# First graph sorted without the nodes' own loops: 440 tiles of edges for 464

## The reference

```python
edge_index = jnp.stack([src, dst])        # 53125, loops among them
# L0: twice GATv2 (4 heads of 64, then 1 of 256), once more with loops appended
src = concatenate([edge_index[0], loops]); dst = concatenate([edge_index[1], loops])
m = xl[src] + xr[dst]; logits = einsum('ehc,hc->eh', leaky_relu(m, 0.2), att)
ex = exp(logits - segment_max(logits, dst)[dst])
out = segment_sum(ex / segment_sum(ex, dst)[dst] * xl[src], dst) + bias
# L1: relations, no loops appended
agg = segment_sum(hx[edge_type, src], dst)
# L2: twice GCN, loops appended: deg counts them
m = (h @ W)[src] * (dinv[src] * dinv[dst])[:, None]; out = segment_sum(m, dst) + b
# L3: 8 heads of 32 with edge attributes, no loops appended
```

## Time and profile before

| what | value |
|---|---|
| median of 3 runs | 9657.73 us (9654.73 to 9668.22) |
| the profiled execution's own time | 9654.4 us |
| its span | 9652.8 us |
| instructions | 96508 |
| mean granted TensorE clock | 0.758 |
| POOL busy, indirect DMAs | 5442.8 us, 56% of the span |
| HBM traffic | 106 GB/s over the span |

### The profile page before, as it was taken

How to read it: one execution, slowest core, us unless ns; L and a number is a source line. 1 busy time by engine, 2 the same in 40 slices (tenths; PEclk the granted TensorE clock), 3 DMA queues, 4 the chain that set the end, 5 groups by cost and what they waited for, 6 DMA issues and landing times. The chain is left out here.

```text
span 9652.8 us, 96508 instructions
## 1 busy us (share of the span) xinstructions
PE 5709.5 (59%) x28237; PEld 4044.7 (42%) x28237; DVE 5273.2 (55%) x11304; ACT 1819.3 (19%) x5534; POOL 5442.8 (56%) x5200
## 2 busy tenths in 40 slices
PE   4866666376665678654687122444444678645496
PEld 4766555254554444443444012333333434334364
DVE  8796566596667852444211196444444455489222
ACT  2444111372110011000111001001000122245110
POOL 2777777374776675576477302774771157546202
PEclk9777889698898989777788556666665555579698
DMA  0001455363555503333456705554552234445311
GB/s 20 4 4 27 126 163 160 98 184 104 161 163 147 148 9 96 99 99 79 130 157 134 77 10 190 149 149 114 150 149 72 70 102 133 119 126 152 108 32 59
DMA packets 570475, 1030.73 MB, mean 107 GB/s; under 512 B 148601, under 2 KB 341795, under 8 KB 568734
## 3 DMA queue, kind: packets, MB, share of 16 engines
q0 software_dynamic: 244320, 586.94, 24.2%
q1 hardware_dynamic: 325657, 437.62, 14.0%
HBM read 812.61 MB, written 211.21 MB: 106 GB/s over the span
## 5 line engine op out<-in xcount | busy, mean ns | idle before, releaser
L171 PE MATMUL ps<-g,oh 128*128 128x256 bf16 (+4 forms) x6496 | 1600.7, 415 | 1313.5 <-issue 796.1
L175 POOL DMA_INDIRECT g<-xl_g,xsrc x1392 | 1531.0, 1100 | 735.8 <-issue 368.0
L171 PEld LDWEIGHTS ps<-g,oh 128*128 128x128 f32 (+1 forms) x6496 | 1143.9, 183 | 1770.0 <-issue 1116.8
L175 POOL DMA_INDIRECT g<-gcn,xsrc x928 | 944.9, 1018 | 855.2 <-SPq L131 571.6
L1188 DVE TENSOR_TENSOR h<-h,ps 128x256 f32 x1392 | 586.3, 421 | 1078.5 <-PE ps L171 903.0
L171 PE MATMUL ps<-g,ident 128*128 128x256 f32 x1856 | 566.6, 459 | 449.8 <-DMA g<-xl_g,xsrc 449.6
L175 POOL DMA_INDIRECT wide<-gat_rows,xs x576 | 575.6, 999 | 356.1 <-issue 174.6
L181 POOL DMA_INDIRECT tab_m<-x,m_addr x441 | 493.0, 1118 | 288.8 <-DVE m_addr L612 154.8
L181 POOL DMA_INDIRECT tab_n<-n_pay,n_addr x537 | 537.0, 1000 | 203.5 <-issue 163.3
L171 PEld LDWEIGHTS ps<-g,ident 128*128 128x128 f32 x1856 | 396.4, 224 | 569.9 <-DMA g<-xl_g,xsrc 510.9
L175 POOL DMA_INDIRECT g<-hx_rel,xtyp x464 | 475.2, 1024 | 252.6 <-issue 141.2
(11 more groups left out here) (499 smaller groups left out, 10700.9 us busy)
## 6 DMA issues: line engine op xcount, KB each, us to landing
kept_g<-g SPq DMA_DIRECT2D x232, 256.0 KB, 2.2
g<-kept_g SPq DMA_DIRECT2D x232, 256.0 KB, 3.2
rowb<-dst_rows_m SPq DMA_DIRECT2D x87, 512.0 KB, 4.5
kept_h<-gk SPq DMA_DIRECT2D x116, 264.0 KB, 2.1
g<-kept_h SPq DMA_DIRECT2D x116, 264.0 KB, 2.8
hx_rel<-tb SPq DMA_DIRECT2D x200, 128.0 KB, 1.8
g<-xl_g,xsrc POOLq DMA_INDIRECT x1392
rowb<-dst_rows_n SPq DMA_DIRECT2D x36, 512.0 KB, 4.2
```

The costliest lines, as they stand in the source:

```text
L171: return k.nc.tensor.matmul(out, lhsT, rhs, start=start, stop=stop, skip_group_check=True)
L175: return k.nc.gpsimd.indirect_dma_start(out=out, out_offset=None, in_=table, in_offset=bass.IndirectOffsetOnAxis(ap=index, axis=0), bounds ...
```

## The change

The loops that L0 and L2 append are no longer edges of m: J is 416 and T 440. What they contributed is computed per node:

- GCN sums start from the node's own row: `gcn_table` keeps dinv x h in `h` and `seg_sum(begun=True)` adds to it, without its memset. The degree is the count plus 1.
- GATv2: `gat_tables` keeps xl in the output tile and writes xl + xr over xT; `gatv2_logits` makes the nodes' own logits of it, in 20 pieces of VectorE work per layer, one in every fifth group of tiles. The softmax now stores each edge's maximum, not the difference; `numerators` takes the place of `from_rows` and also keeps that maximum M per edge; `seg_mean` sums H more columns with it (weighed by the numerators, or with one head in the one-hots), gets the node's maximum by division, and joins both shares (`with_own`).
- The softmax of m works on TS = 448 columns, 8 of them with a target that matches none, in 32 windows of 14 tiles per head (29 of 16 before), 112 with one head (116), 16 with eight.
- `dlR` and `loopneg` are gone.

The second graph's lists stay; its softmax goes through `numerators` too.

```diff
 def both_graphs(k, a, x):
-    m = EdgeList(k, "m", 441, 464, 8)
+    m = EdgeList(k, "m", 416, 440, 8)
+    k.TS = 448
...
 # seg_softmax, sync
-            sp.dma_start(dram2.rearrange("(q e) -> q e", q=Q), x[0:Q, :])...
+            sp.dma_start(dram2.rearrange("(q e) -> q e", q=Q), d[0:Q, 0:n])...
 # seg_softmax, vector
-            vec.tensor_tensor(x[0:Q, :], x[0:Q, :], d[0:Q, 0:n], ALU.subtract)...
...
-    from_rows(k, dram2, H * T, L, ACT.Exp)
+    numerators(k, dram2, H * T, L, M, M is not None and H > 1)
 # numerators, ACT and VectorE (new; loads and transposes as from_rows)
+            for i in range(n + 2):
+                if i < n and M is not None:
+                    act.wait_ge(turned.sem, turned.at(i + 1))
+                    act.copy(M[:, cols(i)], k.ps[i % 4][:, 0:widths[i]])...
+                if i >= 2:
+                    act.wait_ge(shifted.sem, shifted.at(a + 1))
+                    act.activation(L[:, cols(a)], L[:, cols(a)], ACT.Exp)...
+            for i in range(n + 4):
+                if i < n:
+                    vec.tensor_tensor(L[:, cols(i)], L[:, cols(i)], maxima, ALU.subtract)...
+                if i >= 4 and weigh:
+                    vec.tensor_tensor(M[:, cols(a)], M[:, cols(a)], L[:, cols(a)], ALU.mult)
 # seg_sum
-            step(k, vec.memset(acc[:, :], 0.0))
+            if not begun:
+                step(k, vec.memset(acc[:, :], 0.0))
 # seg_mean, ACT, per group
+                if own is not None:
+                    act.copy(g[:, rows_at(t, S), D + H:V], mv[:, t:t + S, :])
 # seg_mean, with_own, after eleven small operations and one Exp
+            if H == 1:
+                for b in range(NB):
+                    vec.wait_ge(own_weighed.sem, own_weighed.at(b + 1))
+                    vec.scalar_tensor_tensor(out=o3[:, b, :], in0=a3[:, b, 0:D], scalar=both[:, 0, b, :],
+                                             in1=o3[:, b, :], op0=ALU.mult, op1=ALU.add)
+                return
+            for h in range(H):
+                for s, v3 in enumerate((a3, o3)):
+                    v = v3[:, :, c * h:c * (h + 1)]
+                    step(k, vec.tensor_tensor(v, v, bc(both[:, s, :, h:h + 1], [128, NB, c]), ALU.mult))
+            vec.tensor_tensor(o3, o3, a3[:, :, 0:D], ALU.add)
 # gatv2_logits, vector
+                if i % 5 == 4 and i // 5 < 20:
+                    own_logits(i // 5 // 4, i // 5 % 4)
+        def own_logits(s, part):
+            v = sums[:, :, 640 * s:640 * (s + 1)]
+            if part == 0:
+                step(k, vec.scalar_tensor_tensor(out=v, in0=v, scalar=0.2, in1=v, op0=ALU.mult, op1=ALU.max))
+            elif part == 1:
+                chain(k, vec.tensor_tensor, v4, v4, bc(att...), ALU.mult)
+            else:
+                chain(k, vec.tensor_reduce, own[...], v[:, part - 2, :]..., AX, ALU.add)
 # gat_tables, vector, per block of the right-hand projection
+                    vec.tensor_tensor(xT[:, :, 128 * i:128 * i + 128], h3[:, i, :]..., ps(NB + i)..., ALU.add)
 # gcn_table, vector, per block
-                    vec.scalar_tensor_tensor(out=rest[:, i % 4, :], in0=k.ps[2 + i % 4][:, 0:D],
-                                             scalar=dinv[:, i:i + 1], in1=buf[:, i % 6, 0, :], ...)
+                    vec.tensor_scalar(h3[:, i, :], k.ps[2 + i % 4][:, 0:D], dinv[:, i:i + 1], None, ALU.mult)
+                    vec.tensor_tensor(rest[:, b % 4, :], h3[:, b, :], buf[:, b % 6, 0, :], ALU.subtract)
 # l3_logits
-            chain(k, vec.tensor_tensor, Lv, Lv, bc(k.loopneg[:, :].unsqueeze(1), [128, 8, T]), ALU.add)
```

More of the change, by code:

```diff
@@ L303, in split_digits @@
         made = sum(len(lists) for _, lists, _, _ in graphs) + 1
+        with_loops = [e.name for e, _, loops, _ in graphs if loops is not None]
         def sync():
@@ L318, in pool @@
             for e, _, loops, _ in graphs:
+                if loops is None:
+                    continue
                 nc.gpsimd.wait_ge(loaded[e.name].sem, loaded[e.name].at(len(parts[e.name])))
@@ L334, in vector @@
             vec.wait_ge(cleared.sem, cleared.at(made))
-            for i, (e, _, _, attr) in enumerate(graphs):
+            for e, _, loops, attr in graphs:
                 vec.wait_ge(loaded[e.name].sem, loaded[e.name].at(len(parts[e.name])))
-                vec.wait_ge(looped.sem, looped.at(2 * i + 2))
+                if loops is not None:
+                    vec.wait_ge(looped.sem, looped.at(2 * with_loops.index(e.name) + 2))
                 digits(e, cols[e.name], ti[e.name], attr)
@@ L734, in vector @@
             vec.tensor_copy(k.attr[:, :, :], p[:, :, 4:7])
[L735 to L738 removed]
+            vec.scalar_tensor_tensor(out=k.dlA[:, :], in0=k.blk[:, :], scalar=-128.0, in1=p[:, :, 0], op0=ALU.mult,
+                                     op1=ALU.add)
         sync()
@@ L934, in scans @@
             step(k, vec.tensor_copy(cc[0:Q, 0:1], k.ps[0][0:Q, 0:1]))
-            chain(k, vec.tensor_tensor_scan, o, g, i_, cc[0:Q, 0:1], ALU.add, ALU.max)
+            if back:
+                after_steps(k, vec)
+                vec.tensor_tensor_scan(o, g, i_, cc[0:Q, 0:1], ALU.add, ALU.max).then_inc(maxima_made.sem,
+                                                                                          maxima_made.up())
+            else:
+                chain(k, vec.tensor_tensor_scan, o, g, i_, cc[0:Q, 0:1], ALU.add, ALU.max)
         def vector():
@@ L1135, in is_kept, with seg_sum @@
     return t % 4 >= 2
-def seg_sum(k, T, table, rows, idx, dl, offs, acc, W=D, parts=1, S=8, R=4):
+def seg_sum(k, T, table, rows, idx, dl, offs, acc, W=D, parts=1, S=8, R=4, begun=False):
     nc = k.nc
@@ L1204, in seg_sum, with seg_mean @@
         fence(k)
-def seg_mean(k, T, table, dl, ex, out, H, kept, W=D, least=1.0e-30):
+def seg_mean(k, T, table, dl, ex, out, H, kept, W=D, least=1.0e-30, M=None, own=None):
     nc = k.nc
     vec, act, pe, gp, sp = nc.vector, nc.scalar, nc.tensor, nc.gpsimd, nc.sync
-    S, R, V = 4, 4, D + H
+    S, R, V = 4, 4, D + H * (1 if own is None else 2)
     G = T // S
+    TS = ex.shape[1] // H
     on_act = {1: 0, 4: 2, 8: 1}[H]
@@ L1228, in seg_mean @@
         ones_set = k.sem("ones_set")
+        shifted, powered = k.sem("logits_shifted"), k.sem("numerators_made")
+        shares, own_weighed = k.sem("shares_made"), k.sem("own_weighed")
+        a3 = acc[:, 0, :].rearrange("p (b c) -> p b c", b=NB)
+        o3 = out.rearrange("p (b c) -> p b c", b=NB)
+        c = D // H
         def rows_at(t, n=1):
@@ L1376, in of, with gatv2_logits @@
         return self.oh[:, (t // 4) % self.R, 128 * (t % 4):128 * (t % 4) + 128]
-def gatv2_logits(k, T, table, xr3, att, H, L, kept):
+def gatv2_logits(k, T, table, xr3, att, H, L, kept, sums, own):
     nc = k.nc
@@ L1456, in vector @@
         def vector():
+            vec.memset(Lv[:, T:, :], 0.0)
             for i in range(4):
@@ L1488, in gatv2_logits, with gat_tables @@
         fence(k)
-def gat_tables(k, xT, Wl, Wr, att, xr3, attb, table):
+def gat_tables(k, xT, Wl, Wr, att, xr3, attb, table, h3):
     nc = k.nc
@@ L1559, in gat_layer @@
 def gat_layer(k, name, xT, Wl, Wr, att, H, acc):
-    T = k.T
+    T, TS = k.T, k.TS
     table = k.dram("xl_" + name, (3200, D))
@@ L2657, in gcn_table @@
         loaded, projected, taken = k.sem("weights_loaded", 16), k.sem("projected"), k.sem("projected_kept")
-        part_a, part_v = k.sem("parts_kept_a"), k.sem("parts_kept_v")
+        first, second, third = k.sem("first_parts_kept"), k.sem("second_parts_kept"), k.sem("third_parts_kept")
+        rests = k.sem("rests_made")
         stored = k.ring("table_stored", 6)
```

308 lines of the change are left out of this document (184 added, 124 removed).

## The result

| | before | changed |
|---|---|---|
| median | 9658.75 us (9654.73 to 9668.22, 4 runs) | 9343.6 us (9337.72 to 9347.09, 4 runs) |
| profiled execution (span) | 9654.4 us (9652.8) | 9347.09 us (9345.8) |
| mean granted TensorE clock | 0.758 | 0.759 |

The ratio is 0.9672, with a 95% interval of 0.9655 to 0.9688: the change is faster by 3.3%, 315 us by the medians, 307 by the profiled executions. 9365 was forecast, with 9333 to 9398 as the range. Four kernels of the experiments ran first in a period when the chip granted TensorE less clock (0.706 on average for 0.759), in which the kernel before took 11229.75 us.

The account below looks back on a forecast made before the run. The prediction took POOL, issuing one indirect DMA per tile, to bound the first graph's tile stages, with no engine bounding the whole span. Its terms summed to -292 us from 9657.7, giving 9365 us, range 9333 to 9398.

Parts of the forecast that it names:

- Start: Before layer 0: 25 fewer scatters and a first address 9 us earlier bring the first gather to about 1002.6, -42.5 us.
- Logits: Layer 0's two logits passes: 24 fewer tiles at 1.413 us each, -67.8; nodes' own VectorE pieces slow POOL, +11.
- Sums, means, last logits: First graph's passes: 24 fewer tiles at POOL's price; plain sums -95.4, means' gathers -51.6, last layer's logits -36 us.
- Rival (e): First graph's stages: latency, not POOL's rate, sets a group's pace, so they win a third less, 70 us: 9435; chance 0.04.
- Softmaxes: All softmaxes: new windows cut load waits and stores, subtractions go, numerators cost +3, +2.5, +1, +1; sum -56 us.
- Tails: Behind the means' last tiles: joining the nodes' own shares costs +17.8 with four heads, +8.2 with one, +26 us together.
- Tables: Projections and GCN tables: extra VectorE operations cost +7 in the second layer and +6.5 per GCN table, +20 us.
- the fixed price of the product: Logits passes: two-SBUF-input VectorE work, judged from the product r x attb, costs POOL 0.36 us per us.
- (a): New VectorE work locks POOL out for its full length: own logits cost 30, tables and tails 10 more: 9395; chance 0.10.
- (b): Start does not follow: late sort-to-tables chain or address only 3 us earlier; first gather wins 25: 9382; chance 0.10.
- (c): Cheaper outcome: the softmax wins 58, tails and tables cost two thirds: 9345; chance 0.14.
- (d): Logits stages and means: changed rhythm leaves TensorE at its lower clock, 0.50, costing 578 us: 9943; chance 0.02.

## Why the prediction held, point by point

**Start, -42.5: -35.2 in the profile shown, about -40 as a rule.** The 25 scatters gave what was said. The first address was to come 9 us earlier; the first scatter came 0.9 earlier in the profiled execution, 7 to 9 in most others (164 to 166 for 172.8 and 173.5). The tables were ready at 995.2, 996 was forecast: that is luck, since the forecast counts on the 9 us that didn't come in this execution. Where the address came early the tables were ready at 980 to 984, so this chain was put some 14 us too late. POOL stayed last, by 15 us instead of 7 in the profiled execution and by some 23 in the others (last scatter at 1003 to 1006); the run with fewer scatters shows that these microseconds can be had.

**Logits, -67.8 + 11: -66.9.** The own pieces cost 9 to 15 us in the passes against the kernel without them, so that term was right. That the passes still lost nearly all of 67.8 comes from the other side: the product with att held gathers for 108 and 117 ns on average over all gathers in the two passes of the kernel before, and for 98 and 105 now. The step that failed is the belief that a duration from one execution has a fixed price in it; the share of gathers caught moves with the rhythm, by some 5 us per pass.

**Sums, means, last logits: -183 forecast, -178 measured.** The prices per tile came out within 0.005 us. Rival (e), latency, is out: 24 tiles less shortened these stages by nearly 24 prices of POOL, not by two thirds of them. (The kernel with 464 tiles agrees, with 208 us for 195 in the six passes, but part of that is the empty tiles' own slowness.)

**Softmaxes, -56: -68.** The mechanism was right (17.9 us of wait for 20 forecast, store 3.7 for 4.6). Mis-sized was the cost of the numerators, 7.5 in all: with four heads it is 12.4 us from the first load to the next gather, for 12.6 before, where I had added 3, and with one head 5.3 for 4.8, where I had added 2.5. So the four-head part won 52.5 instead of 48. That with one head won 6.3 instead of 1: besides its wait (8.3 us for 11.9, as forecast) its store became shorter too (2.3 us to the next load for 4.8), which was in no term. With eight heads it was 7.0, in the second graph 2.5.

**Tails, +26: +24.** The eight products took 14.0 us in a row (14.1 forecast), the sum 6.82. With one head the 25 operations took 9.98 us in one row for 12.1: I had taken 0.484 from an operation that reads PSUM.

**Tables, +20: +14.** The projections cost 3.5 us for 7; the GCN tables 5.8 and 5.0 for 6.5. Why the projections cost half was not looked into.

**What the sum owes to luck.** The total, -307 for -292, is nearer than its terms: the logits passes and softmaxes won 22 us more than forecast and tails and tables cost 8 less, while start, sums, means and the rest fell 15 short. No term is off by more than some 12 us, but the steps that failed (the fixed price of the product, the numerators, the tables' chain at the start) show in the terms alone.

**The rivals.** (a), a lock for the full length, had the right mechanism and the wrong price: a gather is held for what is left, and most are not held at all. (b) is half there in the profile shown, and by chance of one execution. (c) is nearest in number, 9345: its cheaper softmaxes and tables came, its cheaper tails hardly, and the passes gave the rest. (d): the granted clock stayed at 0.90 in the first pass, and POOL waited for TensorE for 3.0 us of 622. (Its sum is wrong: the stages' figures add up to some 610 us, not 578, which gives about 9975.) How it looks when TensorE gets less is shown by the kernels that ran at 0.706: with 29 windows the first tables were ready at 1633 us instead of 995, and POOL had waits in every pass over the first graph.

## What to carry to other kernels

Where one engine issues a DMA per tile and never waits, the number of tiles times that engine's period, read from one stage's group row, predicts a change to a fraction of a per cent; what then needs thought is what stands around the passes, above all how many windows a load is laid out in. Beside an engine that gathers, an operation with two inputs in SBUF costs by where it stands more than by its length: put it straight behind another of its kind. And padding is not free beyond what hides it: don't walk empty tiles. Letting their rows read different rows may help too; no run here tried it.

## What the runs showed of the hardware

- A gather that starts while VectorE works on two SBUF inputs is held until that operation ends (0.32 us left: 1.19 us long; 0.97 left: 1.84); one that has started is not disturbed, and it doesn't hold VectorE either (1.218 us for the product with or without a gather under way). The same 66 us of such work cost 3.6 or 37.8 us per pass by place.
- Loads in 29 rows of 8 KB move one packet at a time and keep VectorE waiting for 57.5 us; in 28 rows they move 14 and more at a time, and it is 19.4.
- The gathers of empty tiles, whose 128 rows are all the same row, take the DMA engines 0.47 to 0.51 us per packet instead of 0.15 (relation sum). That the sameness is the cause was not tested by itself.
- After a pause of 24 us TensorE ran slowly (2.05 us for a group of matmuls that takes 1.14 later) for 2 to 5 us in nine executions and for 28 us in two, with the same code up to there. The granted clock of those stretches reads 1.00 in both cases, so it doesn't show what slowed them, and what decides between them was not settled.
